# The mixing product of a graph layer: from a pass of its own into the sums of the last edge group, and a binning step cut into pieces

## What is computed

```python
xn = layernorm(x)
msgs = edge_weight[:, None] * xn[dst]
gnn  = segment_sum(msgs, src, 6250)
query, key = xn @ W_qk[0] + b_qk[0], xn @ W_qk[1] + b_qk[1]
value = xn @ W_v + b_v
lam = softmax(key, over nodes).T @ value              # 256 x 256
bn  = lam, normalised per row, times gamma plus beta
x = x + gnn + query @ bn
out = x + moe(layernorm(x))                           # 8 experts, top 2
```

## Time and profile before

| | us |
|---|---|
| median of 3 runs | 1973.59 (1972.01 to 1974.62) |
| the profiled execution | 1980.13 |
| its span in the trace | 1978.4 |
| TensorE busy | 1767.1 (89%) |
| VectorE busy | 1382.4 (70%) |
| GpSimd busy | 1294.9 (65%) |
| ScalarE busy | 1093.5 (55%) |

### The profile page before, as it was taken

The page is one execution under the profiler, slowest core; times in us unless marked ns, Lnnn a source line. Parts: engine busy times, 40 slices in busy tenths (PEclk is TensorE's granted clock), DMA queues, the critical chain, the costliest instruction groups (busy, mean ns, idle before and its releaser), DMA issues. The chain is left out here.

```text
span 1978.4 us, 33519 instructions
## 1 busy us (share of the span) xinstructions
PE 1767.1 (89%) x10522; PEld 1530.3 (77%) x10522; DVE 1382.4 (70%) x2880; ACT 1093.5 (55%) x3267; POOL 1294.9 (65%) x1283
## 2 busy tenths in 40 slices
PE   5778878999899989999999999999999973999994
PEld 3367767988798879888987898788899962887773
DVE  6887579888887888798869886988677767010113
ACT  5542035556555655565556555555566642776672
POOL 1000567777777777777777777777777740777773
PEclk9888989999999999999999999999999986999997
DMA  7523544443233333333333333233344441343557
GB/s 255 188 87 105 188 155 122 147 125 112 90 106 104 108 94 105 104 104 97 107 102 99 102 106 107 91 105 105 103 134 134 136 126 51 105 143 131 164 159 229
DMA packets 130054, 244.30 MB, mean 123 GB/s; under 512 B 26533, under 2 KB 77620, under 8 KB 129880
## 3 DMA queue, kind: packets, MB, share of 16 engines
q0 software_dynamic: 59584, 161.78, 27.2%
q1 hardware_dynamic: 63852, 73.97, 11.5%
q10 hardware_dynamic: 6444, 6.40, 0.9%
HBM read 197.24 MB, written 45.77 MB: 123 GB/s over the span
## 5 line engine op out<-in xcount | busy, mean ns | idle before, releaser
L261 POOL DMA_INDIRECT bins_G<-xn_scratch,bins_row_i x621 | 624.5, 1006 | 190.5 <-issue 182.6
L1412 ACT ACTIVATE edge_weighted<-edge_hots,bins_scale 128x128 f32<-128x128 bf16 x2058 | 638.4, 391 | 53.1 <-DVE edge_row_hots L1469 52.6
L261 POOL DMA_INDIRECT edge_G<-xn_scratch,bins_row_i x408 | 414.5, 1016 | 125.7 <-issue 121.3
L1403 ACT COPY edge_A<-edge_ap 128x384 f32<-128x384 f32 x343 | 164.5, 480 | 528.9 <-PE edge_ap L1362 528.9
L1375 PE MATMUL edge_op<-bins_G,edge_weighted 128*128 128x256 f32 x1242 | 316.3, 391 | 34.7 <-DVE all_xn L1482 21.0
L1464 DVE TENSOR_TENSOR edge_hots<-bins_numbers,bins_recb 128x768 bf16<-128x768 bf16 x343 | 190.7, 556 | 192.6 <-PE edge_ap L1362 186.5
L1362 PEld LDWEIGHTS edge_ap<-edge_weighted,edge_row_hots 128*128 128x128 f32 x2058 | 278.8, 192 | 38.4 <-issue 13.4
L1362 PE MATMUL edge_ap<-edge_weighted,edge_row_hots 128*128 128x128 f32 x2058 | 287.5, 276 | 10.8 <-ACT edge_weighted L1412 7.9
L1379 PE MATMUL edge_op<-bins_win,edge_A 128*128 128x256 f32 x1176 | 289.8, 383 | 0.0
L1375 PEld LDWEIGHTS edge_op<-bins_G,edge_weighted 128*128 128x128 f32 x1242 | 221.4, 191 | 64.2 <-DVE all_xn L1482 26.8
L1379 PEld LDWEIGHTS edge_op<-bins_win,edge_A 128*128 128x128 f32 x1176 | 226.5, 193 | 31.7
(11 more groups left out here) (345 smaller groups left out, 2351.4 us busy)
## 6 DMA issues: line engine op xcount, KB each, us to landing
exp_ys<-ys_scratch SPq DMA_DIRECT2D x12, 1024.0 KB, 6.2
bins_G<-xn_scratch,bins_row_i POOLq DMA_INDIRECT x621
edge_G<-xn_scratch,bins_row_i POOLq DMA_INDIRECT x408
ln_xin<-in_x SPq DMA_DIRECT2D x12, 512.0 KB, 5.4
xn_scratch<-ln_xnb ACTq DMA_DIRECT2D x12, 512.0 KB, 5.9
xnT_scratch<-ln_xT SPq DMA_DIRECT2D x12, 512.0 KB, 6.9
mix_xg<-xn_scratch SPq DMA_DIRECT2D x12, 512.0 KB, 3.8
mix_ek<-xnT_scratch SPq DMA_DIRECT2D x12, 512.0 KB, 5.0
```

The source lines that it names most:

```text
L261: pool.indirect_dma_start(out=self.G[t % self.AHEAD][:, i, :], out_offset=None, in_=xn_dram, in_offset=bass.IndirectOffsetOnAxis(ap=self.r ...
L1403: nc.scalar.copy(A[:, j, :, :].rearrange("p c s -> p (c s)"), ap[j][:, :]).then_inc(a_kept, 1)
L1412: last = nc.scalar.activation(weighted[:, t % 2, i, :], hots[:, t % 2, i // 2, :, i % 2], ACT.Copy, scale=scale[:, b, i:i + 1])
```

## The change

The mixing passes go. `wqbn` and the bias stay in SBUF through the edge stage. In the last edge group (`MIXES` names it for all 49 blocks) PE starts each block's PSUM sum with the mixing product, two fp32 matmuls from a freshly loaded piece of `xnT` (`xs`), and one bf16 matmul of three rows that adds the bias; the bias is split into three bf16 parts for it (`split_bias`, in step 45 of the first group). SP loads each `xs` when the step two before it is done; the two buffers lie in free quarters of two of the G buffers. `h` is loaded with x itself by 13 transfers during the chain of `mix_stage`, and the first `finish` waits for them. The writes to `sum_scratch` go; the fallback now computes its own start.

The binning steps of group 0 that lay in the passes move ahead: steps 8 to 43 lie in the loop of sums (two in each odd round from 3 on), 44 to 48 in the chain, and the decode lies before the last copies of the chain. All five G buffers exist before the edge stage and are filled there. Line 526 is cut into pieces of at most three of its up to eight tables, in all seven groups, and so becomes 14 instructions per group instead of 6.

Of the diff the fallback, the signatures, the calls and part of the removed lines are left out:

```diff
@@ -108,7 +108,8 @@
-    AHEAD, EARLY = 5, 3
+    AHEAD = 5
+    MIXES = [list(range(NB)) if q + 1 == NQ else [] for q in range(NQ)]
@@ -236,7 +237,11 @@
-        self.G = [st.sb(f"G{j}", [P, GN, D]) for j in range(self.EARLY)]
+        self.xg = st.sb("xg", [P, 2, GT, D])
+        self.G = [st.sb(f"G{j}", [P, GN, D]) for j in range(self.AHEAD - 2)] + [self.xg[:, j, 0:GN, :] for j in range(2)]
+        self.xs = [self.xg[:, j, GT - 1, :].rearrange("p (k r) -> p k r", k=KC) for j in range(2)]
@@ -516,7 +521,8 @@
-            for a, b, w in ((0, cut, CB),) if part_ == 0 else ((cut, SP2, CB), (SP2, LP, KG)):
+            parts = ((0, cut, CB),) if part_ == 0 else ((cut, SP2, CB), (SP2, LP, KG))
+            for a, b, w in ((x, min(x + 3, end), w) for first, end, w in parts for x in range(first, end, 3)):
@@ -910,21 +915,13 @@
-        IN_SUMS = {u: [order.pop(0) for _ in range(2 if u in (5, 10, 15) else 1)] for u in range(U)}
-        IN_CHAIN = [[order.pop(0) for _ in range(k)] for k in (0, 0, 2, 1)]
-        IN_MIX = {g: order[g:g + 1] for g in range(NG + 1)}
...
+        IN_SUMS = {u: [order.pop(0) for _ in range(2 if u % 2 and u > 1 else 1)] for u in range(U)}
+        IN_CHAIN = [[order.pop(0) for _ in range(k)] for k in (0, 0, 3, 2)]
@@ -951,17 +948,10 @@
+                sp.wait_ge(exped, NG + 1)
...
-                        sp.wait_ge(mixed, g - 1)
...
-                        sp.wait_ge(h_done, g - 1)
...
-                    sp.dma_start(dst, node_view(x, g, ROWS[g])).then_inc(x_in[g % 2], 16)
+                    dst = h[:, g * GT:(g + 1) * GT, :] if g < NG else h[0:TAIL, g * GT, :]
+                    sp.dma_start(dst, node_view(x, g, ROWS[g])).then_inc(h_in, 16)
@@ -1043,23 +1033,6 @@
-                pe.wait_ge(c, FINAL)
...
-                for g in range(NG + 1):
-                    banks = (kp, mp)[g % 2]
-                    pe.wait_ge(xs_in[g % 2], 16 * (g // 2 + 1))
-                    if g >= 2:
-                        pe.wait_ge(xq_done, g - 1)
-                    for s, r in enumerate(ROWS[g]):
-                        for k in range(KC):
-                            last = nc.tensor.matmul(banks[s // 2][:r, (s % 2) * D:(s % 2 + 1) * D],
-                                                    xs[:, g % 2, k, s * P:s * P + r], wqbn[:, k, :],
-                                                    start=k == 0, stop=k == KC - 1)
-                    last.then_inc(mixed, 1)
-                    if g > 0:
-                        for n in IN_MIX[g - 1]:
-                            bins.pe_share(pe, 0, n)
-                assert not IN_MIX[NG]
@@ -1099,26 +1072,14 @@
-                for g in range(NG + 1):
-                    for n in IN_MIX[g]:
-                        bins.act_share(act, 0, n)
...
-                for t in range(bins.EARLY):
+                for t in range(bins.AHEAD):
+                    if t == bins.AHEAD - 2:
+                        pool.wait_ge(p_used, U)
...
-                pool.wait_ge(exped, NG + 1)
-                pool.wait_ge(c, FINAL)
-                for g in range(NG + 1):
...
-                    pool.wait_ge(xq_done, g + 1)
@@ -1183,30 +1144,14 @@
+                bins.dve_decode(dve, 0)
...
-                for g in range(NG + 1):
...
-                        bins.dve_decode(dve, 0)
-                    dve.wait_ge(x_in[g % 2], 16 * (g // 2 + 1))
-                    dve.wait_ge(mixed, g + 1)
...
-                    last.then_inc(xq_done, 1)
-                    for n in IN_MIX[g]:
-                        bins.dve_share(dve, 0, n)
...
+                nc.vector.tensor_copy(bins.bias, mp[0][0:3, 0:D])
@@ -1281,21 +1230,30 @@
+                def load_xs(i):
+                    if i >= len(mixes):
+                        return
+                    if i >= 2:
+                        q, b = mixes[i - 2]
+                        sp.wait_ge(stepped, q * NB + b + 1)
+                    b = mixes[i][1]
+                    r = rows_of(b)
+                    sp.dma_start(xs[i % 2][:, :, 0:r], xnT_view[:, :, b * P:b * P + r]).then_inc(xs_in[i % 2], 16)
...
+                sp.wait_ge(bias_ready, 1)
+                load_xs(0)
+                load_xs(1)
...
+                for i in range(2, 6):
+                    load_xs(i)
...
+                    load_xs(t + 6)
@@ -1306,9 +1264,8 @@
-                    for t in range(max(q * NB, bins.EARLY), (q + 1) * NB):
-                        if t >= AHEAD:
-                            pool.wait_ge(stepped, t - AHEAD + 1)
+                    for t in range(max(q * NB, AHEAD), (q + 1) * NB):
+                        pool.wait_ge(stepped, t - AHEAD + 1)
@@ -1370,9 +1327,20 @@

+                    mixed = (q, b) in mix_number
+                    if mixed:
+                        i = mix_number[q, b]
+                        if i == 0:
+                            pe.wait_ge(bias_ready, 1)
+                        pe.wait_ge(xs_in[i % 2], (i // 2 + 1) * 16)
+                        for k in range(KC):
+                            nc.tensor.matmul(op[j][:, :], xs[i % 2][:, k, :], wqbn[:, k, :], start=k == 0, stop=False)
+                        nc.tensor.matmul(op[j][:, :], bins.ones[0:3, :], bias_parts[:, :], start=False, stop=False)
...
                     for i in range(GN):
-                        nc.tensor.matmul(op[j][:, :], weighted[:, j, i, :], G[rb][:, i, :], start=i == 0, stop=False)
+                        nc.tensor.matmul(op[j][:, :], weighted[:, j, i, :], G[rb][:, i, :], start=i == 0 and not mixed,
+                                         stop=False)

@@ -1475,11 +1443,30 @@
-                    if q == 0 and b % GT == 0:
-                        g = b // GT
-                        dve.wait_ge(h_saved[g % 4], 16 * (g // 4 + 1))
+                    if q == 0 and b == 0:
+                        dve.wait_ge(h_in, 16 * (NG + 1))
...
+                def split_bias():
...
+                    links = [0]
...
+                    def link(ins):
+                        links[0] += 1
+                        ins.then_inc(split, 1)
+                        dve.wait_ge(split, links[0])
...
+                    rest, parts = bins.bias, bias_parts[:, :]
+                    link(nc.vector.tensor_copy(bins.part16[0], rest))
+                    nc.vector.tensor_scalar(parts, bins.part16[0], ident[0:3, 0:1], None, ALU.mult)
+                    link(nc.vector.tensor_tensor(rest, rest, bins.part16[0], ALU.subtract))
+                    link(nc.vector.tensor_copy(bins.part16[1], rest))
+                    nc.vector.scalar_tensor_tensor(parts, bins.part16[1], ident[0:3, 1:2], parts, ALU.mult, ALU.add)
+                    link(nc.vector.tensor_tensor(rest, rest, bins.part16[1], ALU.subtract))
+                    link(nc.vector.tensor_copy(bins.part16[0], rest))
+                    nc.vector.scalar_tensor_tensor(parts, bins.part16[0], ident[0:3, 2:3], parts, ALU.mult, ALU.add)\
+                        .then_inc(bias_ready, 1)
@@ -1544,6 +1531,8 @@
                             route(b)
+                        if q == 0 and b == NB - 4:
+                            split_bias()
                     if q + 1 < NQ:
...
```

More of the change, by code:

```diff
@@ L882, in mix_stage @@
         rsum = st.sb("rsum", [P, KC])
-        pt = st.sb("pt", [P, PB, 2 * D])
-        M, MT, wqT = [pt[:, k, :].rearrange("p (k d) -> p k d", k=KC) for k in range(3)]
+        MT, wqT = (st.sb(name, [P, KC, D]) for name in ("MT", "wqT"))
+        M = wqbn
+        pt = [a[:, :, :].rearrange("p k d -> p (k d)") for a in (M, MT, wqT)]
+        assert len(pt) == PB
         lam = st.sb("lam", [P, KC, D])
@@ L894, in mix_stage @@
         bqb = st.sb("bqb", [P, KC, P])
[L895 to L898 removed]
+        xg = bins.xg
         kp = [st.ps(f"kp{k}", [P, GROUP]) for k in range(2)]
@@ L912, in mix_stage @@
         xn_in = [st.sem(f"xn_in{j}") for j in range(2)]
-        xs_in = [st.sem(f"xs_in{j}") for j in range(2)]
-        x_in = [st.sem(f"x_in{j}") for j in range(2)]
-        mixed = st.sem("mixed")
-        xq_done = st.sem("xq_done")
-        h_done = st.sem("h_done")
         W_LOADS = 6
@@ L1223, in edge_stage @@
         A = st.sb("A", [P, 2, DN, P])
-        bins.G.extend(st.sb(f"G{j}", [P, GN, D]) for j in range(bins.EARLY, AHEAD))
         G = bins.G
@@ L1246, in edge_stage @@
         win_in = bins.win_in
-        h_saved = [st.sem(f"h_saved{j}") for j in range(4)]
+        xs, xs_in = bins.xs, [st.sem(f"xs_in{j}") for j in range(2)]
+        split, bias_ready = st.sem("split"), st.sem("bias_ready")
+        xnT_view = xnT_dram.rearrange("(c p) n -> p c n", p=P)
+        mixes = [(q, b) for q in range(NQ) for b in bins.MIXES[q]]
+        mix_number = {qb: i for i, qb in enumerate(mixes)}
+        assert len(mixes) == NB
         flag_in = st.sem("flag_in")
@@ L1587, in any_edges_stage @@
         new = st.sb("new", [P, D])
+        ones16 = st.sb("ones16", [3, P], BF16)
+        xs = st.sb("xs", [P, 2, KC, P])
+        xr = st.sb("xr", [P, 2, D])
```

(37 more changed lines are left out.)

72 lines of the change are left out of this document (22 added, 50 removed).

## The result

The changed kernel takes 1984.9 us (median of 4, 1982.43 to 1988.29), the kernel before, measured beside it, 1974.11; the ratio is 1.0058 [1.0044, 1.0072]. In a later round it was 1986.52 against 1975.17, 1.0057 [1.0045, 1.007]. So it is some 11 us slower, where 9 us faster was forecast.

A forecast was written before the change was run, and what follows sets the result against it. TensorE was taken as full in the last edge group, with holes in the six others from waits for VectorE and gathered rows. Terms: -45 - 13 + 48 + 1 = -9 us, so 1964.6 us; range 1950 to 1983.

The forecast's parts named there:

- Part 4: Last edge group: mixing product and bias pass on a full TensorE cost 48 us, between 41 and 60.
- Part 1 and 2: Ahead of the edges: mixing passes go, -56.0 us; binning moved forward costs 11; edges start 45 us earlier (40 to 52).
- Part 3: Six edge groups: line 526 in pieces costs 5 us, saves 18 of 22.6 us row waits; net -13 (-23 to +10).
- Part 5: Small items: splitting the bias in step 45 of the first group, +1 us; filling five gather buffers early, 0.
- The first: Rival, six edge groups: pieces don't free GpSimd, gathers still take over 2.5 us; +9, 1982.6 us; chance 0.17.
- The fourth: Rival: transposed blocks land after more than 6.3 us, or x is late at first addition; +5 to +40; chance 0.08.
- The second: Rival: loop of sums absorbs its waits, edges 50 us earlier, nearly all row waits go; -18, 1955.6 us; chance 0.15.
- the third: Rival, loop of sums: nothing absorbed, sums end 16.3 us later; -4, 1969.6 us; chance 0.16.

The follow-up runs named there:

- before again: The kernel before, unchanged, measured and profiled a second time: 1976.67 us, ratio 1.0003.
- after without pieces: The changed kernel with the long binning product of line 526 whole again, in six instructions per group: 1990.31 us, ratio 1.007.
- old fallback: The changed kernel with the body of the skipped fallback as it was before the change: 1982.87 us, ratio 1.0037.
- pieces alone: The kernel before with line 526 cut into pieces and nothing else of the change: 1967.37 us, ratio 0.9951.
- after again: The changed kernel, unedited, measured and profiled a second time: 1986.52 us, ratio 1.0057.
- bias of 128 rows: The changed kernel with the three-row bias pass made one bf16 pass of 128 rows, 125 of them zero: 1970.62 us, ratio 0.9971.
- the two remedies: The changed kernel with the mixing product spread over edge groups 1 to 5 and the bias added on VectorE: 1951.81 us, ratio 0.9877.

## Why the six groups gained: the clock, not the waits

The row waits went and the waits for VectorE took their place. The six groups as a whole, before and after:

```profile
264.50:1422.60 1158.10, 1094.87 (x6683) 976.83 (x6684) 956.49 (x1851) 668.31 (x2099) 889.23 (x883) 0.98 0.36 108
215.20:1361.90 1146.70, 1085.50 (x6683) 970.04 (x6684) 961.40 (x1907) 668.87 (x2099) 856.90 (x881) 0.99 0.34 103
```

TensorE is idle for 63.2 us before and 61.2 after, but busy for 9.4 us less with the same 6683 products. What changed is its granted clock. The windows of the kernel before around the long products of the third group, and TensorE's waits there (steps 12 to 14):

```profile
704.00:708.00 4.00, 2.76 (x16) 2.34 (x14) 3.96 (x6) 1.20 (x4) 3.39 (x3) 1.00 0.21 61
708.00:712.00 4.00, 3.31 (x11) 2.76 (x12) 3.90 (x10) 1.03 (x4) 2.94 (x4) 0.73 0.34 102
712.00:716.00 4.00, 4.00 (x20) 3.56 (x19) 3.19 (x6) 2.09 (x7) 2.93 (x4) 0.84 0.32 98
```

```profile
698.06 1.56 PE L1375 MATMUL edge_op<-bins_G,edge_weighted 128*128 128x256 f32 x6 [1.26 <-DVE all_xn L1482]
...
703.27 1.53 PE L1375 MATMUL edge_op<-bins_G,edge_weighted 128*128 128x256 f32 x6 [1.68 <-DMA bins_G<-xn_scratch,bins_row_i]
...
708.69 1.75 PE L1375 MATMUL edge_op<-bins_G,edge_weighted 128*128 128x256 f32 x6 [1.93 <-DMA bins_G<-xn_scratch,bins_row_i]
710.24 2.77 PE L1379 MATMUL edge_op<-bins_win,edge_A 128*128 128x256 f32 x6
```

After waits of 1.26, 1.68 and 1.93 us in successive steps the clock stands at its lower level (0.50, 1.2 GHz, in the window from 710 to 712), and six products take 2.77 us instead of 1.46. Steps 11 to 14 of the same group in the changed kernel:

```profile
640.63 1.56 PE L1342 MATMUL edge_op<-bins_xg,edge_weighted 128*128 128x256 f32 x6 [1.20 <-DVE all_xn L1449]
645.55 1.56 PE L1342 MATMUL edge_op<-bins_G,edge_weighted 128*128 128x256 f32 x6 [1.40 <-DVE all_xn L1449]
649.52 1.56 PE L1342 MATMUL edge_op<-bins_G,edge_weighted 128*128 128x256 f32 x6 [0.44 <-DVE all_xn L1449]
654.45 1.56 PE L1342 MATMUL edge_op<-bins_G,edge_weighted 128*128 128x256 f32 x6 [1.40 <-DVE all_xn L1449]
```

They are bound by VectorE, busy for 7.96 of 8 us from 638 to 646, and the clock stays at 1.00. Over steps 11 to 15 TensorE waits about as long in both, 5.8 us before and 5.6 after, but in shorter pieces. Of the eight falls of the clock after the first steps in the first profile of before, five come right behind a wait for rows and three behind a wait of 1.9 us for VectorE; the two of the changed kernel come behind waits for VectorE. Not each such row of waits has a fall behind it: in the second profile of before waits of 1.26, 1.98 and 1.77 us in steps 12 to 14 of the fifth group left the clock at 1.00 (1085 to 1105 us). To see how much the falls cost, I cut the six groups of each profile into 232 windows of some 5 us and added up the clock that was missing, (1 - granted clock, to 0.01) x length:

| kernel | missing clock, us | six groups, us | difference |
|---|---|---|---|
| before | 17.9 | 1158.0 | 1140.1 |
| before again | 16.3 | 1157.8 | 1141.5 |
| after without pieces | 13.6 | 1153.7 | 1140.1 |
| old fallback | 10.3 | 1150.1 | 1139.8 |
| pieces alone | 9.6 | 1147.9 | 1138.3 |
| after again | 8.5 | 1148.5 | 1140.0 |
| after | 6.8 | 1146.7 | 1139.9 |
| bias of 128 rows | 6.8 | 1146.4 | 1139.6 |

The last column is the same to within 3.2 us, while the groups differ by 11.6; the kernels without the bias, without the product and with the bias on VectorE give 1138.3 to 1138.9. So, over these profiles, the shorter holds are worth what they keep of the clock; no run changed the clock alone. It also says where two executions of one kernel part: after and after again differ by 1.7 us of clock and 1.8 us of group. And it bears on the two remedies together: their six groups missed 11.9 us of clock, those with the 128-row pass 6.8. The 5 us of work taken off TensorE and the 5 us of clock lost cancel. Whether that is chance, one profile of each doesn't settle.

## Why the prediction was wrong

- **Part 4 failed, in one term.** It said: "the bf16 pass has no row, lies between 0 and one fp32 pass, and I take 0.15". It measured 0.41 a step, twice the upper bound, and 20 us instead of 7; the product with 42.2 us was right (41). With 0.41 the sum is -9 + 13 = +4 instead of a gain. Of the 20 us between forecast and time 14 lie in the last group, 13 of them in this term, and 5 to 6 between profile and median (last point); the rest cancels. A nearer row was in the trace: an fp32 pass of one row between passes of 128, in the chain. Weight loads of the kernel before:

```profile
189.98 1.36 PEld L1028 LDWEIGHTS mix_mp<-mix_wv,mix_pt 128*128 128x128 f32 x4 [1.85 <-DVE mix_pt L1160]
191.99 0.50 PEld L1030 LDWEIGHTS mix_mp<-mix_bv,mix_ones 1*128 1x128 f32 x2 [0.65 <-issue]
193.13 1.35 PEld L1028 LDWEIGHTS mix_mp<-mix_wv,mix_pt 128*128 128x128 f32 x4 [0.65 <-issue]
```

  There 0.65 us are lost on the way in and 0.65 on the way out, at a granted clock of 0.50; the three-row pass at full clock shows its 0.33 us on the way in alone. I bounded by the number of passes, and the price was in the change between them.
- **Part 1 and 2 held, in part by luck.** First scaling at 197.7 and 199.5 us (191 to 202), 14 later on the mean (11); one-hots at 215 and 217 (220). What lies behind it got 62 us shorter, not 56: the chain took 17.1 us instead of 21.2 (to the last copy), at a clock of 0.80 instead of 0.55, where 0 to 2 had been allowed, and the change of stage 0.3 instead of 1.9. The two misses, 3 and 6 us, went opposite ways, so 48 came out near 45; some 3 of the 6 hang on that clock, which five other kernels with this chain did not have.
- **Part 3 held in size, by another way.** -10.3 for -12, groups of 190.4 to 192.1 us in the first profile (191). The row waits went as forecast, the held gathers took up to 2.0 us and not 1.6. But I had them pass into time one for one; they passed into VectorE's wait, and the gain came by the clock, which the working doesn't mention.
- **Part 5 and the edges' end.** The edit of the fallback, which never runs, stood at nothing; passing it takes 3.4 us more. From the last addition to the end it is 1.1 us more by the profiles, within the 4 us allowed.
- **The rivals.** The first gave 1982.6 us, near the measured time, and its mechanism is false: no gather took 2.5 us. The fourth is false too, no wait for the blocks of `xnT` or for x. The second and the third differ from the forecast in parts 2 and 3 alone and fail with its part 4. None held a price for the bias. The time lies 2 us above the range, whose upper end came from the first rival; the 60 us that part 4 allows for the last group stood in no end of the range, and 62.3 came.
- **From profile to median.** The forecast subtracted a difference worked out on one profiled execution. Before's lay 4 us above its medians and after's 1.5 below, so 5 to 6 of the 11 us stand in no stage of the table, and what they are stays open.

## What to carry to other kernels

Work moved into a stage in which its engine is full costs its whole time there; the same product spread over stages with holes cost 62%. Price each change of a matmul's shape and not only its passes: here a pass of 3 rows between passes of 128 cost 0.41 us, with zeros up to 128 rows 0.11, and on an idle VectorE nothing. Where one wait is taken away, look at what is late next and at the clock in the same steps: 22.6 us of waits went, 20.4 came back from another engine, and the gain went with the clock.

## What the hardware showed

- TensorE: 0.33 us of idleness ahead of a three-row weight load between 128-row ones at full clock, 49 times of 49; none with 128 rows.
- Waits of 1.3 to 1.9 us in successive steps were often, not always, followed by some 3 us at 1.2 GHz, which cost 1.7 us; five of these falls stand at the same place in both profiles of before.
- Passing a skipped body that had grown took 13.3 us instead of 9.9 from the last addition to the next stage, of which some 1 us reached the end by the profiles; which engine's list sets that was not tried.
